# Long convolution on one core: a full float32 matmul per distance against three float32r matmuls of split operands from block 1 on, with the block loads moved ahead in the DMA queue

## What is computed

```python
K = 2.0 * jnp.einsum('hn,hnl->hl', Ct, jnp.exp(P)).real
y = irfft(rfft(u, n=2*L) * rfft(K, n=2*L)[None])[..., :L]      # causal convolution, L = 512
y = (y + u * D[:, None]) * mask[:, None, :]
gate_out = q8(y) @ gate_w.T
up_out = q8(y) @ up_w.T                                        # 512 -> 1376
hidden = jax.nn.silu(gate_out) * up_out
x = x + q8(hidden) @ down_w.T                                  # 1376 -> 512
```

## Time and profile before

| what | value |
|---|---|
| median of three runs | 322.15 us (321.82 to 323.75) |
| the profiled execution's own time | 321.68 us |
| its span in the profile | 319.9 us |
| granted TensorE clock, mean | 0.999 |
| TensorE (PE) busy | 308.4 us, 96% of the span |
| VectorE (DVE) busy | 187.3 us, 59% |
| ScalarE (ACT) busy | 161.3 us, 50% |
| DMA | 38.40 MB, mean 120 GB/s |

### The profile page before, as it was taken

The page is one execution under the profiler, slowest core; times in us unless marked ns, Lnnn a source line. Parts: engine busy times, 40 slices in busy tenths (PEclk is TensorE's granted clock), DMA queues, the critical chain, the costliest instruction groups (busy, mean ns, idle before and its releaser), DMA issues.

```text
span 319.9 us, 4409 instructions
## 1 busy us (share of the span) xinstructions
PE 308.4 (96%) x1561; PEld 162.0 (51%) x1587; DVE 187.3 (59%) x408; ACT 161.3 (50%) x222; POOL 13.7 (4%) x25
## 2 busy tenths in 40 slices
PE   1999999999999999999999999999999999999996
PEld 0467655554455554555455544555455554444443
DVE  6977588475637664465634756375744747433443
ACT  3924556364545364464635546453643646644550
POOL 3031000000001000000001000010001000010010
PEclk9999999999999999999999999999999999999999
DMA  6879999400005570078202680066500770070018
GB/s 200 190 190 230 275 321 328 164 1 2 0 0 101 161 264 2 0 131 299 96 0 36 164 326 0 0 110 235 182 0 0 134 262 0 2 132 0 0 22 243
DMA packets 14013, 38.40 MB, mean 120 GB/s; under 512 B 1470, under 2 KB 6558, under 8 KB 11052
## 3 DMA queue, kind: packets, MB, share of 16 engines
q1 hardware_dynamic: 8412, 26.61, 23.6%
q0 software_dynamic: 5584, 11.57, 20.8%
HBM read 33.93 MB, written 15.81 MB: 155 GB/s over the span
## 4 chain that ended last, share of the span: by engine, by line
PE 93%; DVE 3%; DMA 2%; issue 1%; DVEq 0%; SPq 0%
PE up_ps L588 23%; PE gate_ps L588 23%; PE y_ps L512 22%; PE down_ps L526 17%; PE down_ps L629 1%; PE down_ps L542 1%; PE y_ps L542 1%; PE y_ps L629 1%; DMA toep<-kpad_scratch 1%; DMA prm<-in_params 1%; PE down_ps L466 1%; PE gate_ps L554 1%; PE up_ps L554 1%; DMA kpad_scratch<-hq 1%; DVE xt L902 0%
## 5 line engine op out<-in xcount | busy, mean ns | idle before, releaser
L882 DVE SCALAR_TENSOR_TENSOR hv<-sil,fac,up_ps 128x512 f32<-128x512 f32 (+1 forms) x88 | 65.6, 746 | 116.5 <-PE up_ps L588 86.1
L413 ACT ACTIVATE sil<-gate_ps,fac 128x512 f32<-128x512 f32 (+1 forms) x88 | 60.4, 686 | 128.3 <-PE gate_ps L588 122.5
L588 PE MATMUL up_ps<-yq,wu 128*128 128x512 bf16 (+3 forms) x367 | 88.6, 363 | 0.3
L588 PE MATMUL gate_ps<-yq,wg 128*128 128x512 bf16 (+3 forms) x366 | 88.2, 363 | 0.6 <-DVE hv L882 0.3
L512 PE MATMUL y_ps<-xt,toep 128*128 128x512 f32 (+3 forms) x256 | 80.4, 434 | 0.2 <-DMA toep<-kpad_scratch 0.2
L526 PE MATMUL down_ps<-wd,hq 128*128 128x512 bf16 (+1 forms) x251 | 65.4, 379 | 0.7
L512 PEld LDWEIGHTS y_ps<-xt,toep 128*128 128x128 f32 x256 | 47.2, 190 | 21.5 <-issue 2.9
L588 PEld LDWEIGHTS gate_ps<-yq,wg 128*128 128x128 bf16 x372 | 36.2, 100 | 40.0 <-issue 1.7
L588 PEld LDWEIGHTS up_ps<-yq,wu 128*128 128x128 bf16 x372 | 36.3, 100 | 38.3
L394 ACT ACTIVATE hq<-hv 128x1024 uint16<-128x1024 uint16 (+1 forms) x48 | 46.8, 975 | 0.0
L526 PEld LDWEIGHTS down_ps<-wd,hq 128*128 128x128 bf16 (+1 forms) x264 | 25.9, 98 | 32.5 <-issue 12.6
(11 more groups left out here) (148 smaller groups left out, 99.8 us busy)
## 6 DMA issues: line engine op xcount, KB each, us to landing
xt<-in_xT SPq DMA_DIRECT2D x8, 1024.0 KB, 7.5
out<-in_x SPq DMA_DIRECT2D x7, 1024.0 KB, 5.7
out<-res POOLq DMA_DIRECT2D x7, 1024.0 KB, 7.8
toep<-kpad_scratch SPq DMA_DIRECT2D x6, 1024.0 KB, 10.0
toep<-kpad_scratch SPq DMA_DIRECT2D x8, 256.0 KB, 3.8
wd<-in_down POOLq DMA_DIRECT2D x1, 1280.0 KB, 22.3
xt<-in_x SPq DMA_DIRECT2D x1, 1024.0 KB, 7.4
out<-xt SPq DMA_DIRECT2D x3, 256.0 KB, 3.8
```

Of the source, the lines that this page charges most:

```text
L413: nc.scalar.activation(sil[b][0:w, :], gate_ps[b][0:w, :], ACT.Silu, scale=fac[0:w, S_GATE:S_GATE + 1]).then_inc(silu_done, 1)
L588: mm = nc.tensor.matmul(ps[b][0:w, cols], wt[:, k, c * P:c * P + w], yq[par][:, version, k, cols], start=(k == 0), stop=(k == LB - 1))
L882: v.scalar_tensor_tensor(hv[c // 2 % 3][0:w, c % 2], sil[b][0:w, :], fac[0:w, S_UP:S_UP + 1], up_ps[b][0:w, :], ALU.mult, ALU.mult).then_i ...
```

## The change

Block 0 is computed as before (`conv_first`, toep_a). From block 1 on the operands of distances 0, 1 and 2 are split in two float32r parts, a high part and the rest: the taps once, when they are stored (khigh, klow beside the unsplit kraw), x for each block. Each of these distances takes three float32r matmuls (high taps with high x, high with low, low with high). Distance 3 stays one float32 matmul of unsplit taps (t3) and x. Of each block th, tl (1 MB each) and t3 (256 KB) are loaded, where it was toep (1 MB). ScalarE makes the high part of x (`high_x`, two copies of 128x1024 for a block), VectorE the low part (`low_x`, two subtractions of 128x1024). VectorE copies the taps of groups 1 and 2 and makes their low parts (`low_k`). SyncE's loop is written out, with the loads of block g+3 ahead of the copy of block g+1 and its wait for an addition (`added`). ScalarE's `down_scaled` gets a new count of its semaphore, which names the same copy as before.

```diff
+        toep_a = sb("toep_a", [P, HB, L])
+        th = [sb(f"th{i}", [P, HB, L], F32R) for i in range(2)]
+        tl = [sb(f"tl{i}", [P, HB, L], F32R) for i in range(2)]
+        t3 = [sb(f"t3{i}", [P, HB, P]) for i in range(2)]
+        xh = [sb(f"xh{i}", [P, 2, L], F32R) for i in range(2)]
+        xl = [sb(f"xl{i}", [P, 2, L], F32R) for i in range(2)]
...
-            sp.dma_start(bass.AP(kpad, 0, [[ROW, C], [1, PADK]]), zrow[:, 0:PADK]).then_inc(zeros_in, 16)
+            for k in (kraw, khigh, klow):
+                sp.dma_start(bass.AP(k, 0, [[ROW, C], [1, PADK]]), zrow[:, 0:PADK]).then_inc(zeros_in, 16)
...
             def load_toep(g, par):
-                sp.dma_start(toep[par][:], toep_d[g]).then_inc(conv_in[par], 16)
+                sp.dma_start(th[par][:].bitcast(F32), high_d[g]).then_inc(conv_in[par], 16)
+                sp.dma_start(tl[par][:].bitcast(F32), low_d[g]).then_inc(conv_in[par], 16)
+                sp.dma_start(t3[par][:], raw_d[g, :, :, 3 * P:L]).then_inc(conv_in[par], 16)
...
-                sp.dma_start(bass.AP(kpad, lo * ROW + PADK, [[KB, KA], [ROW, n], [1, KB]]),
-                             krow[:, lo:lo + n, :]).then_inc(k_stored[b], 16)
+                sp.wait_ge(k_copied, 2 * b)
+                sp.dma_start(bass.AP(khigh, lo * ROW + PADK, [[KB, KA], [ROW, n], [1, KB]]),
+                             krow_h[:, lo:lo + n, :].bitcast(F32)).then_inc(k_stored[b], 16)
+                sp.wait_ge(k_split, 2 * b)
+                for table, rows in ((klow, krow_l[:].bitcast(F32)), (kraw, krow)):
+                    sp.dma_start(bass.AP(table, lo * ROW + PADK, [[KB, KA], [ROW, n], [1, KB]]),
+                                 rows[:, lo:lo + n, :]).then_inc(k_stored[b], 16)
...
             store_k(1)
-            sp.wait_ge(k_stored[1], 16)
+            sp.wait_ge(k_stored[1], 48)
             for h in range(HB):
-                sp.dma_start(toep[1][:, h], toep_d[1, :, h]).then_inc(toep_first[HB + h], 16)
+                sp.dma_start(th[1][:, h].bitcast(F32), high_d[1, :, h]).then_inc(toep_first[HB + h], 16)
+                sp.dma_start(tl[1][:, h].bitcast(F32), low_d[1, :, h]).then_inc(toep_first[HB + h], 16)
+                sp.dma_start(t3[1][:, h], raw_d[1, :, h, 3 * P:L]).then_inc(toep_first[HB + h], 16)
             store_k(2)
...
+            for g in range(NBLK - 2):
+                if g + 3 < NBLK:
+                    sp.wait_ge(y_ready, HB * (g + 2))
+                    load_x_t(g + 3, (g + 3) % 2)
+                    load_toep(g + 3, (g + 3) % 2)
+                if g:
+                    sp.wait_ge(added[(g - 1) % 2], 16 * ((g - 1) // 2 + 1))
+                copy_x(g + 1, (g + 1) % 2)
...
-            pool.wait_ge(toep_first[2 * HB - 1], 16)
+            pool.wait_ge(toep_first[2 * HB - 1], 48)
...
+            def high_x(g, par, half, pair):
+
+                at_least(act, xt_in[par], 16 * (half + 1))
+                at_least(act, y_ready, HB * (g - 1) + 2 * pair + 2)
+                nc.scalar.copy(xh[pair][:], xt[par][:, 2 * pair:2 * pair + 2]).then_inc(x_high, 1)
...
+                    elif h == 0:
+                        at_least(pe, conv_in[par], 48 * half)
+                    at_least(pe, x_split, 2 * (g - 1) + h // 2 + 1)
...
                 for d in distances:
+                    if d == 3:
+                        nc.tensor.matmul(y_ps[h % 2][:, 3 * P:L], t3[par][:, h, :], xt[par][:, h, 0:P], start=False,
+                                         stop=False)
+                        continue
+                    for n, (taps, xs) in enumerate(((th, xh), (th, xl), (tl, xh))):
+                        last = nc.tensor.matmul(y_ps[h % 2][:, d * P:L], taps[par][:, h, d * P:(d + 1) * P],
+                                                xs[h // 2][:, h % 2, 0:L - d * P], start=(d == 0 and n == 0),
+                                                stop=(d == 2 and n == 2))
...
+            def low_k(i):
+
+                for half in range(2):
+                    dve.wait_ge(k_copied, 2 * (i - 1) + half + 1)
+                    v.tensor_copy(rows_of_k(i, half), k_in_bank(i, half))
+                    v.tensor_tensor(rows_of_k(i, half, krow_l), k_in_bank(i, half),
+                                    rows_of_k(i, half, krow_h).bitcast(F32), ALU.subtract).then_inc(k_split, 1)
+
+            def low_x(g, pair):
+
+                at_least(dve, x_high, 2 * (g - 1) + pair + 1)
+                v.tensor_tensor(xl[pair][:], xt[g % 2][:, 2 * pair:2 * pair + 2], xh[pair][:].bitcast(F32),
+                                ALU.subtract).then_inc(x_split, 1)
...
+HIGH_PLAN = {4: 0, 8: 1}
+LOW_PLAN = {5: 0, 9: 1}
```

More of the change, by code:

```diff
@@ L151, in adaln_ffn_kernel @@
         krow = inside(hq[1], 6 * JC * KA, C, KB)[0:KA]
+        krow_h, krow_l = (t[0:KA].rearrange("p a b -> p (a b)")[:, 0:C * KB].rearrange("p (c b) -> p c b", b=KB)
+                          for t in (th[0], tl[0]))
         halves = [slice(0, N), slice(N, P)]
@@ L271, in _ @@
             sp.wait_ge(y_ready, HB)
             load_x_t(2, 0)
-            sp.wait_ge(k_stored[2], 16)
+            sp.wait_ge(k_stored[2], 48)
             load_toep(2, 0)
             copy_x(0, 0)
[L276 to L279, removed]
-                    at_least(sp, added[par], 16 * (j + 1))
-                    copy_x(2 * j + 2 + par, par)
-                    next_conv(2 * j + 4 + par, par)
@@ L422, in slots @@
                         code_y(g + 1, 1 - par, CODE_PLAN[c])
+                    if ahead == 2 and c in HIGH_PLAN:
+                        high_x(g + 2, par, half + 1, HIGH_PLAN[c])
                     if c == OUT_SLOTS[-1] and not first:
-                        down_scaled(g - 1, 1 - par, half, HB - 1)
+                        down_scaled(g - 1, 1 - par, half - (1 - par), HB - 1)
             act.wait_ge(scales_ready, 1)
@@ L498, in _, with conv_first @@
             warm(WARM[3])
+            def conv_first(h):
+                pe.wait_ge(toep_first[h], 16)
+                if h == 0:
+                    pe.wait_ge(xt_in[0], 16)
+                at_least(pe, yv_done, h - 1)
+                for d in (0, 1, 3, 2):
+                    last = nc.tensor.matmul(y_ps[h % 2][:, d * P:L], toep_a[:, h, d * P:(d + 1) * P],
+                                            xt[0][:, h, 0:L - d * P], start=(d == 0), stop=(d == 2))
+                last.then_inc(y_ready, 1)
             def conv(g, par, half, h, distances):
@@ L504, in conv @@
                     if isinstance(m, int) and m < 2 * HB:
-                        pe.wait_ge(toep_first[m], 16)
+                        pe.wait_ge(toep_first[m], 48)
                     elif h == 0:
-                        at_least(pe, conv_in[par], 16 * half)
-                    if h == 0:
-                        at_least(pe, xt_in[par], 16 * (half + 1))
+                        at_least(pe, conv_in[par], 48 * half)
+                    at_least(pe, x_split, 2 * (g - 1) + h // 2 + 1)
                     at_least(pe, yv_done, m - 1)
                 for d in distances:
-                    last = nc.tensor.matmul(y_ps[h % 2][:, d * P:L], toep[par][:, h, d * P:(d + 1) * P],
-                                            xt[par][:, h, 0:L - d * P], start=(d == 0), stop=(d == 2))
+                    if d == 3:
[6 more added lines that the diff above has]
+                                                stop=(d == 2 and n == 2))
                 if d == 2:
@@ L922, in slots @@
                         finish_y(g + 1, 1 - par, FINISH_PLAN[c])
+                    if ahead == 2 and c in LOW_PLAN:
+                        low_x(g + 2, LOW_PLAN[c])
                     if c == CH - 1 and ahead == 2:
                         scale_y(g + 2, 0)
+            low_k(1)
             scale_y(0, 0)
-            for h in range(HB):
-                if h < HB - 1:
-                    scale_y(0, h + 1)
-                bound_y(0, 0, h)
-                finish_y(0, 0, h)
+            scale_y(0, 1)
+            bound_y(0, 0, 0)
+            finish_y(0, 0, 0)
+            low_x(1, 0)
+            scale_y(0, 2)
+            bound_y(0, 0, 1)
+            finish_y(0, 0, 1)
+            scale_y(0, 3)
+            bound_y(0, 0, 2)
+            finish_y(0, 0, 2)
+            bound_y(0, 0, 3)
+            finish_y(0, 0, 3)
+            low_x(1, 1)
             scale_y(1, 0)
+            low_k(2)
             dve.wait_ge(k_ready, 2 * len(K_GROUPS))
```

57 lines of the change are left out of this document (27 added, 30 removed).

## The result

The changed kernel takes 329.94 us (median of four runs, 329.46 to 330.40); the kernel before, run beside it, takes 322.02 (321.82 to 323.75). The ratio is 1.0234, with a 95% interval of 1.0195 to 1.0272: slower, 7 us above the forecast of 323 and 1 us beyond the end of its range, 329. The profiled execution took 330.4 us, its span is 328.4.

What follows compares the result with a forecast made beforehand. TensorE's matmuls were taken to bound the kernel from block 1 on, DMA loads the start. Tables landing at 61.5 + 259.5 after them + 1.4 for the clock = 322.4 us; median 322.9, said as 323, range 314 to 329.

Steps and rivals of the forecast that it cites:

- landing of block 2's tables: At the start, before block 2's first convolution matmul: th, tl and t3 all loaded at 61.5 us, TensorE waiting 8.5 us.
- gain of 24 channels: TensorE's convolution from block 2 on: each channel 0.48 us shorter with float32r, 11.5 us in all.
- lower clock: TensorE after the wait for block 2's tables: slower matmuls at first, costing about 1.4 us.
- I take the lower one, a gain of 0.48 us a channel: Convolution matmuls: float32r runs at bf16 pace, so a channel takes 1.68 us instead of 2.16; upper bound 3.12.
- The argument from four products: Convolution matmuls: float32 takes four column times as four products of halves; a float32r matmul is one of those products.
- two column times: Rival, convolution matmuls: a float32r matmul takes as long as one float32 record; 357 us, chance 0.08.
- the pace of the weight load: Rival, convolution matmuls: none shorter than its 190 ns weight load, losing 0.33 of the 0.48 us; 331 us, chance 0.06.
- Then th and tl, 1024 packets: Block 2's table loads at the start: alternating packet by packet with wd, they take 10.9 us, until 58.4.
- an idle of 8 us, of the kind that ends at the lower clock: TensorE after waiting for block 2's tables: eight matmuls take 3.18 us instead of 1.73, costing about 1.4.
- The early rival: Start: queues run at the later byte pace, block 2's tables land at 56, wait 3 us; 316 us, chance 0.20.
- The late rival: Start: tap packets alternate with wd or late weights for 7 us, tables land at 66; 327 us, chance 0.14.
- Cost 0, and no gain: SyncE's loop: issuing block g+3's loads earlier changes nothing, since PE waits for no load there today.

Runs made afterwards that it cites:

- e3: The changed kernel with 36 useless matmuls (16 float32r, 20 bf16) filling TensorE's wait before block 2's first convolution matmul; 327.76 us, ratio 1.0180.
- e8: The changed kernel with SyncE's loop in the old order, block g+3's loads behind the copy of block g+1 and its wait for added; 335.7 us, ratio 1.0436.
- e5: The changed kernel with VectorE's low_k(2) moved ahead of low_x(1, 1) and of block 1's first y; 330.56 us, ratio 1.0254.
- e6: The changed kernel with POOL issuing wd only when block 2's three tables have landed; 335.43 us, ratio 1.0427.
- e7: The changed kernel without the load of t3, distance 3 reading th instead; 325.42 us, ratio 1.0148.

## Why the prediction was wrong, point by point

The place and the kind of every term were right: block 2's tables, in turns with wd, and a win in the blocks that the start gives back. Three sizes were off, all the same way, and behind one of them, the landing, a piece of the mechanism was missing. Forecast 322.4 us for the profiled execution, measured 330.4:

| term | forecast | measured | error |
|---|---|---|---|
| landing of block 2's tables | 61.5 | 64.2 | +2.7 |
| gain of 24 channels | 24 x 0.48 = 11.5 | 24 x 0.335 = 8.0 (1.34 for each block of four) | +3.5 |
| lower clock | 1.4 | 3.0 | +1.6 |
| profiled time less its span | 1.8 | 2.0 | +0.2 |

**The matmuls.** This is the step that failed by most: "I take the lower one, a gain of 0.48 us a channel". It measured 0.335. The bf16 pace is a bound that float32r doesn't reach: 0.235, 0.174 and 0.12 us where I had 0.216, 0.162 and 0.108. Part of it, 0.227, shows with ScalarE idle, and with VectorE idle too (e3); what makes up the rest in the blocks was not tried. The argument from four products said how many streams there are, not how fast one is. The two rivals on the pace (two column times, the pace of the weight load) are both refuted: 256 columns take 0.12 us beside a load of 188 ns. The Trainium skill ("FP8 and Floating Point Precision", TensorE Precision Notes) has four passes for true FP32. By that, three passes are three quarters of the time, the 1.68 us of the forecast; the trace shows 1.8.

**The start.** The loads of block 1 were to start at 23.1 and started at 22.26. Block 1's last table was to land near 43; wd, which waits for it, was issued at 45.23. x of block 2 was to be in at 47.5, and moved its last bytes near 48. The step that failed is "Then th and tl, 1024 packets, beside wd's 1376: 470 and 464 packets in 5 us, one for one, so 94 a us, 10.9 us, 58.4". One for one is right (492 to 477), but not from 48 on: until 52 q1 moved 35 packets, where 94 a us make 376, and wd moved 503. tl landed at 62.4, so the two took 14.4 us, 3.5 more than forecast. t3 took 1.8 more, where 58.4 to 61.5 are 3.1. With the 0.5 at the start that makes the 2.7. A hold of this kind stood in the trace of before, but shorter: when x of block 2 had moved its last bytes near 39, q1 moved 12 packets from 39 to 40 and 90 in the next us. The tap stores, 1.5 us in the forecast after 43, landed at 46.8, 2.3 us later than forecast, of which 2 come from block 1's last table.

**The clock.** The step "an idle of 8 us, of the kind that ends at the lower clock, costs about 1.4 once more" took the length of eight matmuls as the length of the lower clock. In the timeline of PE the work from 64.23 to 70.36 us (three float32r matmuls each of 512 and of 384 columns, one of distance 3, eight bf16) took 6.1 us, and takes 3.2 at the later pace. So 3.0 us, and 2.7 to 3.1 by e3. The early rival took nothing for the clock behind its wait of 3 us; behind the wait of 3.5 us in block 1 the granted clock was 0.50.

**The late rival.** It says 327 us and "decides from a landing at 64 on", and the landing was at 64.2. Its mechanism did not come about, though: the tap packets were to alternate with wd or late weights, and from 40 to 45 us q0 moved 52 packets beside q1's 1532, as the forecast had it. That its time is nearer is luck; with its landing of 66 and the gain and the clock as measured it would have come to some 332.

**The rest.** DVE and ACT cost nothing that shows in the blocks (TensorE has no gap), and block 1's own waits, 3.7 us in all where 4 were forecast, were swallowed by the later one. But e8 shows that "Cost 0, and no gain" for the moved loads was wrong: with 2.25 MB a block and a split of x on ScalarE the old order costs 1.2 us a block.

## What to carry to other kernels

When a faster instruction needs more data, ask from which block on it pays. Here each block gains 1.34 us and its loads cost nothing that shows once the weights are in, while the same loads beside the weights cost 2.3 us for block 2 and 7.7 for block 1, where they also push wd into the next tables. Starting at block 3 turned a loss of 2.3% into a win of 1.8%. When queues share the engines, count packets, and count from the first packet, not from the issue. And where two chains end close to each other, shortening one shows only the other (e5).

## What the runs showed of the hardware

- Three float32r matmuls take more than three quarters of the time of a float32 one: about 0.235 us each for 512 columns, against 0.216 for a bf16 one and for a quarter of a float32 one, 9% more.
- A load issued on the hardware queue while the software queue moves wd moves nothing at first. Block 2's tables were issued at 46.8; with x of block 2 ahead of them through near 48, q1 moved 2 packets in each of the stretches 48 to 50 and 50 to 51, 31 in the next us, and had its share from about 53 on. With wd held back (e6), and x landed at the same time, q1 moved 114 packets in the us from 48. The Trainium skill ("DMA: Bandwidth & Descriptors", Latency and other measured facts) has about 0.6 us to the first byte; here th, issued at 46.79, moves its first packets some 4 us later, about 1.5 of them behind x. What holds the load back wasn't tried.
- A small load is dear in turns: 512 packets of 512 bytes in each of two blocks (0.5 MB in all) put block 2 off by 4.7 us (e7), where 0.25 MB a us would make it 2.
